# A decoder layer's attention sums as 64x64 tiles, two jobs moved from VectorE to ScalarE, and the order of all steps written out

## The chip, the cores and the metric

The kernel runs on one core of a Trainium2 chip. The metric is the device time in microseconds (us) of the whole launch. TensorE (PE in the profile) multiplies, VectorE (DVE) and ScalarE (ACT) work elementwise, GpSimd (POOL) does four small operations per norm, and SyncE (SP) issues the transfers.

## The reference, cut to what matters

A post-norm decoder layer on x of (16, 256, 256): three blocks, each `x = layernorm(x + block(x))`.

- **A, attention by moments.** `z = conv(x @ in_proj)`, a causal convolution of 4 taps. The value channels (256 = 32 heads of 8) are multiplied by 4 angles each; cosine and sine of that, times `poly(x) * p * time_weight`, are summed over the sequence (`cumsum`), divided by the summed weight, normalised by their mean square, multiplied by `W_re` and `W_im` (from 8x4 moments back to 8 channels within a head), gated with `silu`, and multiplied by `out_proj`.
- **B, cross attention by autocorrelation.** Fourier transforms of query and context, products, an inverse transform, the top 5 lags of each head and their softmax, applied to the values in the frequency domain.
- **C, feed-forward with 16 small experts.** `xV * cumsum(yW)`, weighted by a softmax over routed experts, times U, divided by the position.

## The kernel before, in words

The batch of 16 is worked off in 8 chunks of 2 sequences: 512 tokens, in tiles of 128 channels by 512 tokens. All of TensorE's large products are in float32; the compiler makes two passes of each (so one product of 512 columns is two MATMUL records).

Every step is a small function (`a_sums`, `b_spectrum`, `c_own`, ...) that exists on each engine that takes part. It waits on semaphores for what it needs and ticks its own; `Steps` counts these. On each engine all steps stand in one order, and an engine works strictly in that order. The order is given by one function `turn` for each engine, which is called NCHUNK + 3 or + 4 times with the chunks a, b, c, d (and e) shifted by one: in turn t it starts block A of chunk t, finishes A of chunk t-1, does B of t-1 and t-2 and C of t-2 and t-3. Below, "turn t" is the stretch from the first transpose of chunk t (`a_transpose(t, 0)`, L540) to that of chunk t+1; the last stretch runs from the transpose of chunk 7 to the end.

Block A has 8 units a chunk (UNITS = 2 halves of 128 channels x M = 4 angles), half by half: unit u is half u // 4, angle u % 4. For each:

- VectorE `a_fraction`: the angle in turns, rounded to an integer by writing it as int32 (`kturn`, L1431), then the fraction left (L1434);
- ScalarE `a_angles`: absolute value, sine, cosine into `sc` (4 slots, cosine and sine of 128x512 each);
- VectorE `a_moments` (times the weight `g`, L1454) and `a_scan` (running sum, L1462);
- TensorE `a_sums` (L585): two products of 128x128 weights `wy` by 128x512 of `sc`, added up in the PSUM bank Y of the half. `wy` is block diagonal, 8x8 for each head;
- ScalarE `a_squares` (L1049), VectorE `a_accumulate` (L1472); then once a chunk TensorE `a_squares` (L597, weights of 128x32), VectorE `a_weight` (L1482), ScalarE `a_norm` (logarithm, exponential, copy), VectorE `a_factor` (L1489), TensorE `a_factor` (L556), VectorE `a_heads`, TensorE `a_out` (L615).

At the end of each block VectorE adds the residual and takes mean and variance, GpSimd makes the reciprocal root (`rstd`, L1259 and L1262), and VectorE subtracts and multiplies in four instructions (`ln_apply`, L1518). TensorE's other large steps: `a_project` (L573), `b_transform` (L631), `b_spectrum` (L647), `b_corr` (L659), `b_back` (L691), `b_out` (L701 and L703), `c_transpose` (L714), `c_hidden` (L724), `c_logits` (L733, weights of 128x32 into two column groups in turn), `c_running` (L758), `c_own` (L767), `c_spread` (L775), `c_out` (L786 and L788). In the first turn TensorE and ScalarE also do 34 `fold` steps (L441, L952), which multiply weight matrices together once; 21 of them stand in one block between `a_project(0, 3)` and `a_sums(0, 0)`.

Of the kernel before, what the change touches and what calls it, by code (L numbers as in the profile page):

```python
# [25 lines left out]
ALU = mybir.AluOpType  # L26
# [25 lines left out]
C_ID, C_HS, C_HM, C_POS, C_RN, C_M0, C_E8, C_SG, C_LO, C_END = 0, 128, 192, 208, 464, 466, 468, 596, 598, 600  # L52
# [29 lines left out]
def each(kinds, over):  # L82
# [3 lines left out]
LAYER_NORM = each("res", range(2)) + each("stats aggr norm", range(NQ))  # L86
# [4 lines left out]
             + each("y", range(UNITS)) + ["S"] + each("fe out", range(2)))  # L91
VEC_A = Steps("vec_a", [("tap", j, t) for j in Z_ORDER for t in (2, 1, 0)] + [("stap", t) for t in (2, 1, 0)]
              + ["clip", "expo", "plow", "den", "guard", "w", "flow"]
              + each("p2 g both gf y", range(2)) + each("turns frac mom scan", range(UNITS))
              + [("acc", u) for u in range(UNITS) if u % M] + LAYER_NORM)
ACT_A = Steps("act_a", each("xT silu p1", range(2)) + ["zs", "exp", "phigh", "e", "ln", "f", "fhigh"]
              + each("z", Z_ORDER) + each("abs cos sin sq", range(UNITS)))
POOL_A = Steps("pool_a", ["var", "rstd"])
# [4 lines left out]
ACT_B = Steps("act_b", each("xf cf ot", range(2)) + SPEC + ["exp", "wt"])  # L103
POOL_B = Steps("pool_b", ["var", "rstd"])
# [6 lines left out]
ACT_C = Steps("act_c", each("xT", range(2)) + each("h", range(4)) + ["logit", "exp", "wT"] + each("c", range(NJ)))  # L111
POOL_C = Steps("pool_c", ["var", "rstd"])
# [5 lines left out]
BANK_A = {("xT", 0): 2, ("xT", 1): 1, ("zs",): 2, ("z", 0): 1, ("out", 0): 0, ("out", 1): 0, ("pe", 0): 2, ("z", 1): 1, ("pe", 1): 2, ("z", 2): 0,  # L118
          ("z", 3): 1, ("Y", 0): 2, ("Y", 1): 0, ("S",): 1, ("fe", 0): 1, ("fe", 1): 1}
# [28 lines left out]
def chunks(t, stages):  # L148

    return [t - n if 0 <= t - n < NCHUNK else None for n in range(stages)]  # L150


# [5 lines left out]
def decoder_kernel(nc, x, ctx_in, in_proj, conv_w, conv_b, theta, decay, anchor, score, deriv, norm_sc,  # L158
# [4 lines left out]
    with ctx:  # L163
# [11 lines left out]
        headm = cst[:, C_HM:C_HM + 16]  # L175
# [5 lines left out]
        psel = sb("psel", [P, 4, P], F32R)  # L181
# [12 lines left out]
        wy = sb("wy", [P, 2, M, P])  # L194
# [62 lines left out]
        rs = [sb(f"rs{n}", [P, 2, NQ]) for n in "abc"]  # L257
# [17 lines left out]
        pselraw = acc[:, 0, 0, :].rearrange("p (k n) -> p k n", n=P)  # L275
# [39 lines left out]
        LOADS_A += [(win[:, :, 0:2 * D], in_proj[:, 0:2 * D].rearrange("(t p) n -> p t n", p=P)),  # L315
                    (wsr[:, :, :], in_proj[:, 2 * D:2 * D + HEADS].rearrange("(t p) n -> p t n", p=P))]
        for j in range(4):
            LOADS_A += [(cw[:, j, :], conv_w[:, 0, j * P:(j + 1) * P].rearrange("a p -> p a"))]
        LOADS_A += [(cb[:, 0:4], conv_b[0:2 * D].rearrange("(t p) -> p t", p=P)),
                    (thn[:, :, :], theta[0, 0].rearrange("(t k) h m -> (k h) t m", t=2)),  # L320
                    ]
# [32 lines left out]
        def _(sp):  # L354
            for dst, src in LOADS_S:
                sp.dma_start(dst, src).then_inc(w_small, 16)
            for dst, src in LOADS_A[:2]:
                sp.dma_start(dst, src).then_inc(w_attn, 16)
            sp.dma_start(xa[:, :, :], rows(x, 0)).then_inc(xa_in, 16)
            for dst, src in LOADS_A[2:]:  # L360
                sp.dma_start(dst, src).then_inc(w_attn, 16)
# [6 lines left out]
            def load_residual(i):  # L368
                if not is_first(i):
                    sp.wait_ge(*VEC_A.at(i - 1, "norm", NQ - 1))  # L370
                sp.dma_start(xs_a[:, :, :], rows(x, i)).then_inc(xr_in, 16)
# [6 lines left out]
            def store(i):  # L378
                sp.wait_ge(*VEC_C.at(i, "norm", NQ - 1))
                sp.dma_start(rows(out, i), xs_c[:, :, :]).then_inc(stored, 16)  # L380
# [15 lines left out]
            for i in range(3, NCHUNK - 1):  # L396
                load_x(i + 1)
                load_residual(i)
                store(i - 3)
                load_ctx(i)  # L400
            load_residual(NCHUNK - 1)
            store(NCHUNK - 4)
            load_ctx(NCHUNK - 1)
            store(NCHUNK - 3)
            store(NCHUNK - 2)
            store(NCHUNK - 1)
# [20 lines left out]
        def _(pe):  # L427
# [126 lines left out]
            def spread_heads(o, h):  # L554
                for b in range(SEQ):
                    last = mm(o[:, b * L:(b + 1) * L], psel[:, 2 * h + b, :], pair[:, :], start=True, stop=True)  # L556
                return last

            @staged
            def a_spread(i, h):  # L560
# [4 lines left out]
                spread_heads(o, h).then_inc(*PE_A.tick("pe", h))  # L565
# [36 lines left out]
            def a_factor(i, h):  # L602
# [4 lines left out]
                spread_heads(o, h).then_inc(*PE_A.tick("fe", h))  # L607
# [13 lines left out]
            def b_transform(i, name, t):  # L621
# [4 lines left out]
                else:  # L626
                    pe.wait_ge(*VEC_A.at(i, "norm", NQ - 1))
# [81 lines left out]
            def c_transpose(i, t):  # L709

                pe.wait_ge(*VEC_B.at(i, "norm", NQ - 1))
# [79 lines left out]
            def turn(a, b, c, d):  # L791
                c_spread(d, 3)
                c_own(d, 3)
                c_running(d, 4)
                b_corr(c)
                a_sums(b, 6)
                if is_first(b):
                    for k in fold_part(6):
                        fold(k)
                c_spread(d, 4)  # L800
                a_sums(b, 7)
                if is_first(b):
                    for k in fold_part(7):
                        fold(k)
                c_own(d, 4)
                c_running(d, 5)
                c_spread(d, 5)
                c_own(d, 5)
                a_squares(b)
                c_running(d, 6)  # L810
                b_wt(c)
                c_spread(d, 6)
                a_factor(b, 0)
                c_own(d, 6)
                b_wf(c)
                a_factor(b, 1)
                a_transpose(a, 0)
                c_running(d, 7)
                c_spread(d, 7)
                a_transpose(a, 1)  # L820
                a_out(b, 0)
                a_scores(a)
                c_own(d, 7)
                a_project(a, 0)
                b_back(c, 0)
                b_back(c, 1)
                a_out(b, 1)
                b_out(c, 0)
                a_spread(a, 0)
                a_project(a, 1)  # L830
                b_out(c, 1)
                c_out(d, 0)
                c_out(d, 1)
                if is_first(b):
                    pe.wait_ge(folded, len(FOLD))
                    pe.wait_ge(ready, 2)
                b_transform(b, "cf", 0)
                a_spread(a, 1)
                a_project(a, 2)
                b_transform(b, "cf", 1)  # L840
                a_project(a, 3)
                if is_first(a):
                    for k in fold_part(None):
                        fold(k)
                c_transpose(c, 0)
                c_transpose(c, 1)
                b_transform(b, "xf", 0)
                b_transform(b, "xf", 1)
# [1029 lines left out]
```

## Time and profile before

| | us |
|---|---|
| three runs | 1075.76, 1076.63, 1078.91 (median 1076.63) |
| the profiled execution | 1077.53 |
| its span, first to last instruction | 1075.7 |
| PE busy (matmuls) | 960.7 (89% of the span) |
| DVE busy | 852.4 (79%) |
| ACT busy | 471.9 (44%) |
| POOL busy | 45.9 (4%) |
| mean granted TensorE clock | 0.963 of full speed |

The span leaves out 1.8 us of the profiled execution's own time; the median of the runs is 0.9 us above the span. Busy times are those of the profile: overlapping instructions of one engine are counted once. The ends of matmuls are modelled, so that a busy PE holds small gaps.

### The profile page before, as it was taken

How to read it: one execution, taken by the hardware profiler on the slowest of the kernel's cores; microseconds unless marked ns; L12 is line 12 of the kernel's file. 1: busy time of each engine (PE TensorE's matmuls, PEld its weight loads, DVE VectorE, ACT ScalarE, POOL GpSimd, SP SyncE). 2: the span in 40 equal slices, each digit the busy share in tenths (PEclk: the TensorE clock that was granted, in tenths of full speed). 3: DMA queues.
4: the chain of work that ended last, by engine and by line, in shares of the span. 5: the costliest groups of instructions: out<-in, count | busy, mean ns of one | idle time of the engine just before them, and what ended most of it. 6: DMA issues, size and time to landing. Idle time of an engine off the chain costs nothing. (4 is left out here: it accounts for less than half of the span.)

```text
span 1075.7 us, 10422 instructions
## 1 busy us (share of the span) xinstructions
PE 960.7 (89%) x3460; PEld 587.8 (55%) x3482; DVE 852.4 (79%) x1459; ACT 471.9 (44%) x736; POOL 45.9 (4%) x64
## 2 busy tenths in 40 slices
PE   2596685889999999999999999999999998998696
PEld 1253352655467545855485547754675467547245
DVE  3769699999997999799989999799979984173232
ACT  1465364268333943285328633583339411410310
POOL 0001000020001000100000000000010001000000
PEclk9799897899999999999999999999999999999789
DMA  7700010010001000010001000100010000000000
GB/s 211 164 1 0 20 39 1 20 39 1 0 21 41 19 1 21 1 59 0 20 1 59 1 0 21 59 1 1 1 52 8 1 1 20 1 0 1 19 1 20
DMA packets 38167, 25.45 MB, mean 24 GB/s; under 512 B 17991, under 2 KB 37474, under 8 KB 38114
## 3 DMA queue, kind: packets, MB, share of 16 engines
q1 hardware_dynamic: 38114, 24.78, 8.0%
q8 instruction: 29, 0.48, 0.2%
q14 instruction: 24, 0.20, 0.1%
HBM read 20.58 MB, written 4.19 MB: 23 GB/s over the span
## 5 line engine op out<-in xcount | busy, mean ns | idle before, releaser
L1462 DVE TENSOR_TENSOR_SCAN sc<-mask,sc 128x1024 f32<-128x1024 bf16 x64 | 146.2, 2284 | 0.1
L585 PE MATMUL ps<-sc,wy 128*128 128x512 f32 x256 | 126.2, 621 | 13.5 <-DVE sc L1462 10.8
L767 PE MATMUL ps<-x2t,mv 128*128 128x512 f32 x256 | 122.5, 601 | 3.2 <-DVE prod L1707 3.1
L758 PE MATMUL ps<-cum,mw 128*128 128x512 f32 x256 | 123.6, 606 | 1.2 <-ACT wparts L1136 1.2
L786 PE MATMUL ps<-up,prod 128*128 128x256 f32 x512 | 115.9, 379 | 0.9 <-DVE prod L1707 0.9
L786 PEld LDWEIGHTS ps<-up,prod 128*128 128x128 f32 x512 | 94.8, 190 | 13.8 <-issue 1.7
L1145 ACT ACTIVATE cs<-ps 128x512 f32<-128x512 f32 x64 | 37.7, 589 | 113.3 <-PE ps L758 112.5
L1454 DVE TENSOR_TENSOR sc<-sc,g 128x1024 f32<-128x1024 f32 x64 | 77.6, 1212 | 9.7 <-ACT sc L1030 9.5
L585 PEld LDWEIGHTS ps<-sc,wy 128*128 128x128 f32 x256 | 48.0, 195 | 66.0 <-issue 50.2
L758 PEld LDWEIGHTS ps<-cum,mw 128*128 128x128 f32 x256 | 47.5, 192 | 60.1 <-issue 59.7
L1375 DVE SCALAR_TENSOR_TENSOR zc<-ps,cw,zc 128x510 f32<-128x510 f32 (+2 forms) x96 | 71.0, 745 | 11.2 <-ACT zc L971 8.9
L767 PEld LDWEIGHTS ps<-x2t,mv 128*128 128x128 f32 x256 | 47.4, 191 | 57.6 <-issue 47.3
L573 PE MATMUL ps<-xt,win 128*128 128x512 f32 x128 | 67.3, 654 | 0.0
L1072 ACT ACTIVATE spec<-ps 128x512 f32<-128x512 f32 x32 | 18.8, 595 | 109.5 <-PE ps L631 109.2
L1699 DVE TENSOR_TENSOR cs<-cs,ps 128x512 f32<-128x512 f32 x64 | 43.6, 681 | 24.3 <-ACT cs L1145 14.6
L724 PE MATMUL ps<-x2t,mr 128*128 128x512 f32 x128 | 60.0, 614 | 0.8 <-ACT x2t L1105 0.8
L1049 ACT ACTIVATE sq<-sc 128x1024 f32<-128x1024 f32 x48 | 50.5, 1051 | 21.2 <-DVE sc L1462 21.2
L1472 DVE TENSOR_TENSOR acc<-acc,sq 128x1024 f32<-128x1024 f32 x48 | 58.6, 1220 | 0.6 <-ACT sq L1049 0.3
L1716 DVE SCALAR_TENSOR_TENSOR x<-ps,cst,x 128x256 f32<-128x256 f32 x32 | 14.0, 480 | 55.5 <-PE ps L788 55.5
L971 ACT ACTIVATE zc<-ps,cb,cw 128x512 f32<-128x512 f32 x32 | 24.8, 775 | 64.2 <-PE ps L573 64.1
L1707 DVE TENSOR_TENSOR prod<-cs,ps 128x512 f32<-128x512 f32 x64 | 43.7, 683 | 10.3 <-PE ps L767 9.9
L1019 ACT ACTIVATE hq<-frac 128x512 f32<-128x512 f32 x64 | 40.1, 627 | 23.6 <-DVE frac L1434 23.4
(253 smaller groups left out, 1628.3 us busy)
## 6 DMA issues: line engine op xcount, KB each, us to landing
xa<-in_x_dram SPq DMA_DIRECT2D x8, 512.0 KB, 3.9
xs_a<-in_x_dram SPq DMA_DIRECT2D x8, 512.0 KB, 3.8
cin<-in_ctx_dram SPq DMA_DIRECT2D x8, 512.0 KB, 5.6
out_dram<-prod SPq DMA_DIRECT2D x8, 512.0 KB, 4.8
win<-in_L_attn_in_proj_w_dram SPq DMA_DIRECT2D x1, 512.0 KB, 4.1
prod<-in_L_ffn_V_fwd_dram SPq DMA_DIRECT2D x2, 256.0 KB
prod<-in_L_ffn_W_fwd_dram SPq DMA_DIRECT2D x2, 256.0 KB
prod<-in_L_ffn_W_inv_exp_dram SPq DMA_DIRECT2D x2, 256.0 KB
```

Source lines behind the costliest of these rows:

```text
L573: last = mm(o, win[:, t, j * P:(j + 1) * P], xt[:, t, :], start=(t == 0), stop=(t == DT - 1))
L585: last = mm(y, wy[:, 1 - c, m, :], sc[:, u % 4, c, :], start=(m == 0 and c == 0), stop=(m == M - 1 and c == 1))
L724: last = mm(o, mr[:, t, br, r * P:(r + 1) * P], x2t[:, t, :], start=(t == 0), stop=(t == 1))
L758: last = mm(o, mw[:, t, br, c:c + P], cum[:, t, :], start=(t == 0), stop=(t == 1))
L767: last = mm(o, mv[:, t, br, c:c + P], x2t[:, t, :], start=(t == 0), stop=(t == 1))
L786: mm(d, prod[:, j, q * P:(q + 1) * P], up[:, j, :], start=(j == 0), stop=False)
L1049: A(dst, sc[:, u % 4, :, :], ACT.Square, scale=1.0 / math.sqrt(2.0 * HD * M))\
L1375: STT(o[:, :, s:L], z[:, :, 0:L - s], cw[:, j, tap:tap + 1], o[:, :, s:L], ALU.mult, ALU.add)\
L1454: TT(sc[:, s, :, :], sc[:, s, :, :], g[:, h, :].unsqueeze(1).broadcast_to([P, 2, T]), ALU.mult)\
L1462: V.tensor_tensor_scan(flat, mask[:, 0:2 * T], flat, 0.0, ALU.mult, ALU.add)\
L1472: TT(acc[:, h, :, :], acc[:, h, :, :], sq[:, u % 2, :, :], ALU.add).then_inc(*VEC_A.tick("acc", u))
L1707: TT(prod[:, j, :], cs[:, j % 2, :], ps[:, BANK_C[("x", j)], :], ALU.mult)\
```

## The change

1. **Sums as tiles.** `a_sums` takes an angle m of both halves at once: 8 products of 64x64 weights by 64x512, in the four quadrants of TensorE's array, instead of 4 products of 128x128. It runs 4 times a chunk instead of 8. The channel quarters are placed so that the lower 64 rows always write the bank of Y 0 and the upper 64 rows that of Y 1. Units are counted angle by angle (u = 2m + h), and the first half holds channel quarters 0 and 3, the second 1 and 2. The loads of `win`, `cw`, `cb` and `thn` are cut into pieces for that, and a second selection matrix `pouter` is made.
2. **Integer turns on ScalarE.** `kturn` is written by an ACTIVATE (Identity with a scale column) in the new `a_turns`; VectorE keeps the second half of `a_fraction`.
3. **The norms' last step on ScalarE.** `ln_apply` becomes four ACTIVATE (Identity, bias and scale columns) in `a_layer`, `b_layer`, `c_layer`; GpSimd makes the bias as well, four operations in place of two. Waits on "norm" go to ScalarE's semaphores.
4. **One order for all chunks.** `turn` is gone on each engine. All steps of all eight chunks are written out, in an order that differs from chunk to chunk; the folds are spread among them. SP's order of transfers stays nearly the same.

```diff
             @staged
-            def a_sums(i, u):
-                h, m = divmod(u, M)
-                if m == 0:
-                    free_a(i, "Y", h)
-                y = ps[:, BANK_A[("Y", h)], :]
-                pe.wait_ge(*VEC_A.at(i, "scan", u))
-                for c in range(2):
-                    last = mm(y, wy[:, 1 - c, m, :], sc[:, u % 4, c, :], start=(m == 0 and c == 0),
-                              stop=(m == M - 1 and c == 1))
-                last.then_inc(*PE_A.tick("y", u))
+            def a_sums(i, m):
+                if m == 0:
+                    free_a(i, "Y", 0)
+                    free_a(i, "Y", 1)
+                pe.wait_ge(*VEC_A.at(i, "scan", 2 * m))
+                pe.wait_ge(*VEC_A.at(i, "scan", 2 * m + 1))
+                for c in range(2):
+                    for h in range(2):
+                        for r in range(2):
+                            src, dst = slice(r * H, (r + 1) * H), slice((r ^ h) * H, ((r ^ h) + 1) * H)
+                            last = mm(ps[dst, BANK_A[("Y", r)], :], wy[src, 1 - c, m, :], sc[src, (2 * m + h) % 4, c, :],
+                                      start=(m == 0 and c == 0), stop=(m == M - 1 and c == 1))
+                last.then_inc(*PE_A.tick("y", m))
...
+            @staged
+            def a_turns(i, u):
+                m, h = divmod(u, 2)
...
+                if u >= 2:
+                    act.wait_ge(*ACT_A.at(i, "cos", u - 2))
...
+                A(kturn[:, u % 2, :], zc[:, h, :], ACT.Identity, scale=thn[:, h, m:m + 1]).then_inc(*ACT_A.tick("turns", u))
...
+            def ln_apply(i, k, xs, dst, OWN, POOL):
+                act.wait_ge(*POOL.at(i, "rstd", 3))
+                for q in range(NQ):
+                    A(dst[:, q, :], xs[:, q, :], ACT.Identity, bias=rs[k][:, 2, q:q + 1], scale=rs[k][:, 1, q:q + 1])\
+                        .then_inc(*OWN.tick("norm", q))
...
             def a_fraction(i, u):
-                TS(kturn[:, u % 2, :], zc[:, h, :], thn[:, h, m:m + 1], None, ALU.mult)\
-                    .then_inc(*VEC_A.tick("turns", u))
-                dve.wait_ge(*VEC_A.at(i, "turns", u))
+                dve.wait_ge(*ACT_A.at(i, "turns", u))
                 STT(frac[:, u % 2, :], zc[:, h, :], thn[:, h, m:m + 1], kturn[:, u % 2, :], ALU.mult, ALU.subtract)\
                     .then_inc(*VEC_A.tick("frac", u))
...
-            def ln_apply(i, k, xs, dst, VEC, POOL):
-                dve.wait_ge(*POOL.at(i, "rstd"))
-                for q in range(NQ):
-                    TS(dst[:, q, :], xs[:, q, :], mvr[k][:, q, 0:1], rs[k][:, 1, q:q + 1], ALU.subtract, ALU.mult)\
-                        .then_inc(*VEC.tick("norm", q))
```

On TensorE the new order around the end of chunk 6's block A is this (the same sort of place in each of chunks 3 to 6):

```
... c_running(4, 7) c_spread(4, 7) c_own(4, 7) a_sums(6, 1) b_back(5, 0) b_back(5, 1) c_out(4, 0) c_out(4, 1)
a_sums(6, 2) a_sums(6, 3) a_squares(6) b_out(5, 0) a_factor(6, 0) b_out(5, 1) a_factor(6, 1)
a_transpose(7, 0) a_transpose(7, 1) a_out(6, 0) a_scores(7) a_project(7, 0) b_transform(6, "cf", 0) a_out(6, 1) ...
```

and at the end: `... c_out(6, 0) c_out(6, 1) b_out(7, 0) b_out(7, 1) c_transpose(7, 0) ...`. In the first turn 9 folds stand before `a_sums(0, 0)` on TensorE, and on ScalarE 7 stand before `a_angles(0, 2)`, where it was all of the first 21.

## Rows read from the trace of the kernel before

**Rows 1.** The page: busy time of each engine, and TensorE's in 40 slices

```profile
PE 960.7 (89%) x3460; PEld 587.8 (55%) x3482; DVE 852.4 (79%) x1459; ACT 471.9 (44%) x736; POOL 45.9 (4%) x64
PE   2596685889999999999999999999999998998696
```

**Rows 2.** Windows by turn: length, busy time (and instructions) of each engine, clock

```profile
20.20:112.70 92.50, 68.27 (x201) 36.32 (x201) 66.84 (x86) 46.90 (x85) 5.41 (x5) 0.89 0.31 73
112.70:198.50 85.80, 60.69 (x196) 37.03 (x197) 77.15 (x111) 40.70 (x63) 1.22 (x2) 0.84 0.06 19
198.50:301.50 103.00, 96.32 (x336) 56.47 (x337) 97.92 (x157) 57.03 (x87) 5.58 (x4) 0.97 0.05 16
529.70:643.80 114.10, 111.71 (x420) 68.98 (x422) 104.31 (x177) 57.69 (x88) 4.80 (x6) 1.00 0.06 19
757.90:1075.70 317.80, 287.97 (x1063) 181.56 (x1069) 185.02 (x368) 94.60 (x145) 12.23 (x18) 0.96 0.03 11
```

**Rows 3.** Timeline, TensorE: start, length, then line, operation, shape and count

```profile
512.27 1.05 PE L659 MATMUL ps<-fidft,cspec 128*32 128x256 f32 x4
...
520.65 1.88 PE L767 MATMUL ps<-x2t,mv 128*128 128x512 f32 x4
...
522.46 1.06 PE L597 MATMUL ps<-acc,cst 128*32 128x256 f32 x8
...
523.46 1.98 PE L758 MATMUL ps<-cum,mw 128*128 128x512 f32 x4
```

**Rows 4.** The chain that ended last: start, length, what

```profile
1012.55 1.91 PE ps L733 x8
...
1032.84 1.72 PE ps L758 x4
...
1052.03 3.69 PE ps L786 x16
...
1067.44 0.89 DVE x L1716 x2
```

**Rows 5.** Groups by line and form, VectorE: busy, mean ns, idle before

```profile
L1431 DVE TENSOR_SCALAR hq<-zc,thn 128x512 int32<-128x512 f32 x64 | 30.8, 481 | 0.3
...
L1518 DVE TENSOR_SCALAR prod<-x,mvrc,rsc 128x256 f32<-128x256 f32 x32 | 11.1, 410 | 11.2 <-POOL rsc L1262 11.2
```

**Rows 6.** Groups by line and form, ScalarE

```profile
L1000 ACT ACTIVATE g<-zc,dw 128x512 f32<-128x512 f32 x16 | 12.9, 805 | 3.0 <-DVE zc L1375 3.0
...
L948 ACT ACTIVATE up<-ps,acol 128x256 f32<-128x256 f32 x4 | 1.9, 474 | 5.0 <-PE ps L441 5.0
```

**Rows 7.** Groups by line and form, GpSimd

```profile
L1262 POOL TENSOR_TENSOR rsc<-rsc,half_ 128x4 f32<-128x4 f32 x8 | 8.1, 1008 | 0.6
```

**Rows 8.** Waits in the first turn (20 to 112.7 us): us in total, times, longest

```profile
DVE sc L1454 <- ACT sc L1030: 9.5, 1, 9.5
```

**Rows 9.** Timeline: from the squares to the next step, and one `b_out` pair

```profile
525.52 0.42 DVE L1489 TENSOR_TENSOR pair<-den,pair 64x256 fp32r<-64x256 f32 x1
...
526.04 0.51 PE L556 MATMUL ps<-pair,psel 128*128 128x256 f32 x2
...
544.01 1.03 PE L701 MATMUL ps<-wos,spec 128*128 128x256 f32 x4
...
545.97 0.39 PE L556 MATMUL ps<-pair,psel 128*128 128x256 f32 x2
```

**Rows 10.** Timeline, SyncE in the first microseconds, and what VectorE does then

```profile
7.35 0.43 SPq L358 DMA_DIRECT2D win<-in_L_attn_in_proj_w_dram  x1
...
8.85 3.09 SPq L361 DMA_DIRECT2D cw<-in_L_attn_conv_w_dram  x4
...
11.98 1.10 SPq L361 DMA_DIRECT2D cb<-in_L_attn_conv_b_dram  x1
...
13.12 0.51 SPq L361 DMA_DIRECT2D thn<-in_L_attn_theta_dram  x1
...
15.38 0.17 DVE L1323 TENSOR_SCALAR thn<-thn 128x8 f32<-128x8 f32 x1
```

**Rows 11.** Timeline, TensorE before the last chunk's block C

```profile
999.26 1.97 PE L714 MATMUL ps<-cst,x 128*128 128x128 f32 x8 [6.49 <-DVE x L1518]
```

More of the change, by code:

```diff
@@ new lines, in _ @@
+            b_wt(0)
+            b_wf(0)
+            a_sums(1, 1)
+            a_sums(1, 2)
+            b_back(0, 0)
+            b_back(0, 1)
+            b_out(0, 0)
+            a_sums(1, 3)
+            b_out(0, 1)
+            a_squares(1)
+            a_factor(1, 0)
+            a_factor(1, 1)
+            a_transpose(2, 0)
+            a_transpose(2, 1)
+            a_out(1, 0)
+            a_scores(2)
+            a_out(1, 1)
+            a_project(2, 0)
+            c_transpose(0, 0)
@@ new lines, in _ @@
+            c_spread(1, 4)
+            c_own(1, 4)
+            b_wt(2)
+            b_wf(2)
+            c_running(1, 5)
+            c_spread(1, 5)
+            c_own(1, 5)
+            c_running(1, 6)
+            b_back(2, 0)
+            b_back(2, 1)
+            c_spread(1, 6)
+            c_own(1, 6)
+            c_running(1, 7)
+            a_sums(3, 1)
+            c_spread(1, 7)
+            c_own(1, 7)
+            b_out(2, 0)
+            b_out(2, 1)
+            c_out(1, 0)
+            c_out(1, 1)
@@ new lines, in _ @@
+            b_wt(3)
+            c_own(2, 5)
+            c_running(2, 6)
+            c_spread(2, 6)
+            b_wf(3)
+            c_own(2, 6)
+            c_running(2, 7)
+            a_sums(4, 1)
+            c_spread(2, 7)
+            c_own(2, 7)
+            b_back(3, 0)
+            b_back(3, 1)
+            c_out(2, 0)
+            c_out(2, 1)
+            a_sums(4, 2)
+            a_sums(4, 3)
+            a_squares(4)
+            b_out(3, 0)
+            a_factor(4, 0)
+            b_out(3, 1)
@@ new lines, in _ @@
+            b_wf(4)
+            c_own(3, 6)
+            c_running(3, 7)
+            c_spread(3, 7)
+            c_own(3, 7)
+            a_sums(5, 1)
+            b_back(4, 0)
+            b_back(4, 1)
+            c_out(3, 0)
+            a_sums(5, 2)
+            c_out(3, 1)
+            b_out(4, 0)
+            b_out(4, 1)
+            a_sums(5, 3)
+            a_squares(5)
+            b_transform(5, "cf", 0)
+            b_transform(5, "cf", 1)
+            a_factor(5, 0)
+            a_factor(5, 1)
@@ new lines, in _ @@
+            c_spread(4, 7)
+            c_own(4, 7)
+            a_sums(6, 1)
+            b_back(5, 0)
+            b_back(5, 1)
+            c_out(4, 0)
+            c_out(4, 1)
+            a_sums(6, 2)
+            a_sums(6, 3)
+            a_squares(6)
+            b_out(5, 0)
+            a_factor(6, 0)
+            b_out(5, 1)
+            a_factor(6, 1)
+            a_transpose(7, 0)
+            a_transpose(7, 1)
+            a_out(6, 0)
+            a_scores(7)
+            a_project(7, 0)
@@ new lines, in _ @@
+            c_own(6, 6)
+            c_running(6, 7)
+            b_back(7, 0)
+            c_spread(6, 7)
+            c_own(6, 7)
+            b_back(7, 1)
+            c_out(6, 0)
+            c_out(6, 1)
+            b_out(7, 0)
+            b_out(7, 1)
+            c_transpose(7, 0)
+            c_transpose(7, 1)
+            c_hidden(7, 0)
+            c_hidden(7, 1)
+            c_hidden(7, 2)
+            c_hidden(7, 3)
+            c_logits(7)
+            c_running(7, 0)
+            c_turn(7)
@@ L1241, in _ @@
+            c_logits(7)
+            c_exp(7)
+            c_weights(7)
+            c_tile(7, 0)
+            c_tile(7, 1)
+            c_tile(7, 2)
+            c_tile(7, 3)
+            c_tile(7, 4)
+            c_tile(7, 5)
+            c_tile(7, 6)
+            c_tile(7, 7)
+            c_layer(7)
         @block.gpsimd
```

2200 lines of the change are left out of this document (1820 added, 380 removed).

## The prediction, made before the changed kernel ran

> **What bounds the kernel now.** I read the page first. TensorE is busy 960.7 of 1075.7 us, VectorE 852.4 [rows 1]. TensorE's slices show where that share is an average: below 9 in the first eight slices and in some of the last seven, full in between [rows 1]. So I cut the span by turns and asked for the windows [rows 2]. The reader is to see three kinds of stretch.
>
> - The first two turns (92.5 and 85.8 us): TensorE 68.3 and 60.7 us busy, and that at a granted clock of 0.89 and 0.84; VectorE 66.8 and 77.2. No C work exists yet. VectorE with its waits sets the length.
> - The steady turns, four of 114.1 us (the one from 529.7 stands for them): TensorE 111.7 busy, VectorE 104.3, ScalarE 57.7. TensorE is the bound, idle 2.4 us a turn; VectorE has only 9.8 us of slack.
> - The last stretch, 317.8 us: TensorE 288.0 busy, VectorE 185.0. TensorE is idle 29.8 us, all of it in pauses between dependent steps.
>
> A microsecond taken from TensorE therefore counts in the turns from 198.5 on, one taken from VectorE in the first two.
>
> **The sums, before.** Two products are four passes of 512 columns, and four such passes take 1.72 us (L758) [rows 4]. A chunk has 8 units: 13.7 us of its 111.7.
>
> **The sums, after.** No row shows four quadrants at work, nor two row halves. What rows show is two column groups. `c_logits` has 8 passes of 512 columns with 32-column weights, in two column groups in turn, and takes 1.91 us (L733) [rows 4]: the time of four passes, not eight. `a_squares` has 8 passes of 256 columns, first the four of one group, then the four of the other, and takes 1.06 us, where `b_corr`'s 4 passes in one group take 1.05 [rows 3]. So column groups run fully side by side, each with its own moving data, whatever their order in the program. The new group is 16 passes over four quadrants, four in each: at least 1.72 us if all four run together; 3.44 if only two do; 6.88 if none. The number of instructions is hardly a limit: in those 1.06 us TensorE takes 8 loads and 8 matmuls, and at that rate 16 and 16 need 2.1 us, no more than I come to below. I take 1.72, by the nearness of the column rows.
>
> Going in and out of a tiled group costs. Between the start of L767 at 520.65 and the first pass of L758 after the tiled L597 (523.46, and 0.10 more, since its four took 1.98 instead of 1.88) lie 2.91 us, for four passes of 512 (1.72) and the time of four of 256 (0.86): 0.33 us lost [rows 3]. A new group costs 1.72 + 0.33 = 2.05, four a chunk 8.2. Gain: 13.7 - 8.2 = 5.5 us; as `a_sums(2)` and `a_sums(3)` stand together in the new order and share one switch, I take 5.7.
>
> The Trainium skill ("TensorEngine Tiling (Array Packing)", Key Properties) agrees that a change of tiling mode drains the engine and that 64x64 gives four independent tiles; its Gotcha 1 says that two row tiles can't write one PSUM bank at a time. Here the lower rows write only bank Y 0 and the upper ones only Y 1, so by that page nothing is in the way. Against the change speaks "TensorE: Matmul & The Clock Gate" (Part 3): matmuls start and end in strict program order. What that would make of the time is a rival below; the `a_squares` row, where the second group does not wait for the first one's four passes, does not bear it out.
>
> **VectorE.** The integer turns are 64 instructions with 30.8 us, 3.85 a turn; the norms three groups of 32 with 11.1, 11.0 and 11.0, 4.1 a turn [rows 5]. VectorE has 104.3 - 8.0 = 96.3 us a turn left.
>
> **ScalarE.** The turns become ACTIVATEs of 128x512. The nearest row with columns for scale and bias takes 805 ns (L1000) [rows 6]; 8 a turn are 6.4 us, and at the lowest nothing more than VectorE's 481 ns each, 3.8. The norms are 12 ACTIVATEs of 128x256 at some 474 ns (L948) [rows 6], 5.7 us. From 57.7 to about 70 of a turn: it doesn't bound. This is costed at nothing because ScalarE idles 56 us a turn; without that cover it would be 12 us a turn. What can show is latency: the last fraction of each unit now needs one ScalarE step more, queued among copies out of PSUM. There are two slots, and fractions stand two units ahead of the moments in both orders, so in a turn I cost it at 0, at most 0.8 a unit, 6 a turn.
>
> **GpSimd** makes two operations more per norm. The power takes 1.0 us [rows 7]; the two new ones multiply only, between 0.2 and 1.0 each. Norms of A and of most of B are covered by other TensorE work; the last B and the last C are not.
>
> **The order, steady turns.** C of a chunk now ends before the next transpose of A; before, its last experts, `c_out`, and B's `b_back` and `b_out` lay in the next turn. Per turn the work is the same: 111.7 - 5.7 = 106.0 us. Does the new order starve TensorE at the end of A, where less C is left to fill? From the squares (522.46) to the factor product (526.04) the round trip through VectorE and ScalarE takes 3.6 us [rows 3, 9]. Behind the squares now stands only `b_out(5, 0)`, 1.96 us (544.01 to 545.97) [rows 9], and the squares themselves take 1.06: about 0.6 us is left open, before `a_squares` perhaps as much for the last three accumulates. I take the idle time of before, 2.4, and 0.6: a turn of 109.0. Bounds: 106.6 (the join hidden) and 114.
>
> **The start.** The first transpose waits for VectorE's setup, which has to wait for the small loads: it reads `thn` at 15.38, the queue having issued the last at 13.12 [rows 10]. SP now issues `win` in four pieces (+3 x 0.43), `cw` in five (+0.8), `cb` in four, `thn` in three (+2 x 0.51), nine issues more. For `cb` I take four small ones of about 0.45 for one of 1.10, +0.7. Together +3.8; the smaller `wy` gives 0.3 back. First transpose at 20.2 + 3.5 = 23.7 (bounds 20.2, if the loads weren't late, and 26).
>
> **First turn.** 3.85 us of integer turns leave VectorE. VectorE also stood 9.5 us before a moment [rows 8], while ScalarE copied the block of 21 folds. With 7 folds ahead of `a_angles(0, 2)` most of that goes; what is late next is ScalarE itself, which has 47 + 6 us to do. I take 5.4 of it: 92.5 - 3.8 - 5.4 = 83.3 (bounds 79 and 92).
>
> **Second turn.** VectorE loses 5.2 us (turns, one norm), and gains the end of B (0), which lay in the next turn (`b_apply`, `b_mix`, residual, about 7). 85.8 + 1.2 = 87 (83 to 92).
>
> **Third turn.** It now holds all of C (0), like a steady one: 109, where it was 103.
>
> **The last stretch.** It no longer holds what of C (4) and B (5) was left at the transpose of chunk 7: one expert step (1.72 x 2 + 0.2), `c_out` from 1052.0 to 1067.4 [rows 4], `b_back` (16 passes of 256 columns, 3.5 as such passes of L786 take), `b_out` 2 x 1.96: 26.4 us. The sums give 5.7. The norm before the last C has a pause of 6.5 us already [rows 11], in which VectorE waited for `c_out(6)`; now it follows `b_out(7)` and is residual, statistics, GpSimd and four ACTIVATEs, about the same. The end: two GpSimd operations and slower norms, +2 in all. 317.8 - 26.4 - 5.7 + 2.3 = 288.0.
>
> **Sum.** 23.7 + 83.3 + 87 + 5 x 109 + 288 = 1027.0 us of span, against 1075.7. The runs' median stands 0.9 above the span, the profiled time 1.8: **1028 us** for the median, -4.5%.
>
> **Rivals.**
>
> - **Coupling (0.12).** The chain of A's steps sets the turn, not TensorE's sum: fractions late by ScalarE, accumulates late before the squares. For: VectorE's 96.3 us leave 10 to 13 of slack, queues are strict. Against: before, with 9.8 of slack, TensorE idled 2.4. At turns of 114, 5 x 5: 1053.
> - **Two quadrants at a time (0.07).** Only column groups overlap, row halves don't. Group 3.44 + 0.33: 1.72 more, 24 groups in the TensorE-bound turns (chunks 2 to 7): +41, 1069.
> - **Strict order (0.04).** Each product is two passes in one quadrant; if passes start in program order, a product's second pass holds up the next quadrant. Nine steps of 0.43 = 3.9 us and 0.33, 2.2 more than forecast: +52, 1080, no change. That would be the page's rule quoted above.
> - **One at a time (0.07, the case of slower).** If 64-row weights stop the overlap altogether, a group takes 6.88 + 0.33, 5.2 more: 24 x 5.2 = +124, 1152 us. From a group of about 4.1 us on (49 us of gain over 24 groups are 2.0 each) the change no longer pays. No row excludes it; the column rows speak against.
>
> **Numbers.** The forecast has 0.70; its own range is 1010 to 1044, from turns at 106.6 (-12) and first turns at their low bounds (-6), to turns of 111 (+10) and the others high. The range of 8 in 10 goes to 1062: it takes in coupling, not the quadrant rivals. A change within 0.3% can't be told from none here. Faster 0.89 (forecast, coupling, two at a time), same 0.04, slower 0.07.
>
> **What would show it.** Sums: the group of 16 passes in 1.7 to 2.1 us on the timeline; 3.4 or 3.9 or 6.9 name the rivals. Steady windows of 107 to 111 us with TensorE near 106 and VectorE near 96; if TensorE's busy time falls but the turn stays, it is coupling, and the waits before L597's and the sums' successors name the place. The first transpose near 23.7. VectorE's wait of 9.5 us gone. The last stretch near 288. The prediction is wrong if the sums don't overlap, or if the written-out order makes pauses that the join's arithmetic above doesn't see.

## The result, and the profile after

The changed kernel takes 1031.15 us (four runs, 1029.45 to 1032.04) against 1077.2 for the kernel before beside it: a ratio of 0.957, 95% interval 0.9549 to 0.9591. The forecast was 1028. The profiled execution has a span of 1030.3 us.

The page of the changed kernel: busy times, TensorE's slices, and the groups that answer to the changed lines.

```profile
PE 911.1 (88%) x3719; PEld 553.9 (54%) x3738; DVE 792.5 (77%) x1301; ACT 565.7 (55%) x902; POOL 44.7 (4%) x112
PE   0489945889999999989998999989999999999795
L610 PE MATMUL ps<-sc,wy 64*64 64x512 f32 x512 | 62.7, 614 | 2.6 <-DVE sc L2539 2.6
L1537 ACT ACTIVATE hq<-zc,thn 128x512 int32<-128x512 f32 x64 | 46.0, 721 | 5.2 <-DVE zc L2460 4.1
```

Against [rows 1] TensorE has lost 49.6 us of busy time, VectorE 59.9, and ScalarE has gained 93.8. The sums are now 512 passes, twice as many as the 256 before, with a busy time of 62.7 us in all (a "pass" is one MATMUL record); the slices look as they did, low at the start, full in the middle.

The windows, in the order of [rows 2]: the first two turns, turns three to seven in one row, the last stretch. TensorE's new line for the transpose is L562.

```profile
24.00:103.50 79.50, 60.47 (x233) 31.39 (x233) 62.31 (x78) 49.27 (x89) 0.00 (x0) 0.89 0.37 86
103.50:192.60 89.10, 60.41 (x264) 39.24 (x265) 77.34 (x108) 52.21 (x83) 4.11 (x9) 0.83 0.06 18
192.60:752.70 560.10, 536.93 (x2248) 328.71 (x2262) 483.05 (x763) 346.17 (x540) 22.22 (x56) 0.99 0.06 19
752.70:1030.30 277.60, 252.58 (x976) 154.09 (x980) 161.84 (x310) 116.18 (x186) 16.09 (x36) 0.97 0.04 12
```

| stretch | predicted | measured |
|---|---|---|
| to the first transpose | 23.7 | 24.0 |
| first turn | 83.3 | 79.5 |
| second turn | 87 | 89.1 |
| five turns | 545 | 560.1 |
| last stretch | 288 | 277.6 |
| span | 1027.0 | 1030.3 |

The last two rows must be read together. The new order does not repeat from chunk to chunk, and the transpose that I cut at stands at a slightly different place in each; the single turns are 113.0, 112.2, 107.7, 119.2 and 108.0 us. Over both stretches TensorE is busy 789.5 us where I had 786, and idle 48.2 where I had 47. The five turns alone have 6.9 us of busy time more than 5 x 106.0, and most of that is the clock. In the kernel before the steady turns stand at a granted clock of 1.00; here it is at the lower of its two levels in three stretches of these turns (193.0 to 196.4, 223.8 to 227.3 and 558.3 to 565.2), in which TensorE is busy 12.8 us. The last of them, with what TensorE did ahead of it:

```profile
554.25 1.89 PE L672 MATMUL ps<-wqs,spec 128*128 128x256 f32 x8
559.30 2.07 PE L672 MATMUL ps<-wks,spec 128*128 128x256 f32 x4 [3.16 <-ACT qkv L1604]
...
558.30:565.20 6.90, 5.90 (x15) 4.82 (x16) 6.83 (x6) 3.19 (x6) 0.00 (x0) 0.51 0.00 0
```

TensorE stood idle for 3.2 us from 556.1 on, and at the lower level four passes then take 2.07 us where eight took 1.89. Half of the 12.8 us, 6.4, is my estimate of what the lower clock adds to the busy time of the five turns.

The timeline of TensorE at two groups of sums: one alone between full products, two together ahead of the squares.

```profile
490.97 1.88 PE L783 MATMUL ps<-cum,mw 128*128 128x512 f32 x4
492.78 1.95 PE L610 MATMUL ps<-sc,wy 64*64 64x512 f32 x16
494.88 1.88 PE L792 MATMUL ps<-x2t,mv 128*128 128x512 f32 x4 [0.16 <-issue]
...
515.31 3.66 PE L610 MATMUL ps<-sc,wy 64*64 64x512 f32 x32
519.06 1.06 PE L622 MATMUL ps<-acc,cst 128*32 128x256 f32 x8
```

Sixteen passes of 512 columns end after 1.95 us, where four of 128x128 take 1.88: all four quadrants run at once. From the start of the group to that of the next full product are 2.10 us; two groups in a row take 3.66. The forecast said 1.72 and 0.33, together 2.05.

### The profile page after: what moved, and what is told of

Its sections match the earlier page's. It is cut to its first block, busy times and chain, and to the rows that moved or that the text cites. A ratio compares the mean times of both kernels' runs of the same rounds, so it can differ in the third digit from the quotient of the medians.

```text
span 1030.3 us, 11040 instructions
## 1 busy us (share of the span) xinstructions
PE 911.1 (88%) x3719; PEld 553.9 (54%) x3738; DVE 792.5 (77%) x1301; ACT 565.7 (55%) x902; POOL 44.7 (4%) x112
## 4 chain that ended last, share of the span: by engine, by line
PE 64%; DVE 15%; ACT 13%; issue 5%; SPq 1%; POOL 1%; DMA 0%; ACTq 0%; DVEq 0%; POOLq 0%
PE ps L811 9%; PE ps L792 9%; PE ps L783 9%; PE ps L672 7%; PE ps L610 4%; PE ps L595 3%; PE ps L640 3%; PE ps L716 3%; PE ps L463 3%; PE ps L656 3%; DVE zc L2460 2%; PE ps L726 2%; DVE sc L2539 2%; ACT x L1674 2%; ACT L1422 1%
## 5 line engine op out<-in xcount | busy, mean ns | idle before, releaser
L2460 DVE SCALAR_TENSOR_TENSOR zc<-ps,cw,zc 128x510 f32<-128x510 f32 (+2 forms) x96 | 71.3, 743 | 22.7 <-ACT zc L1484 20.3
L610 PE MATMUL ps<-sc,wy 64*64 64x512 f32 x512 | 62.7, 614 | 2.6 <-DVE sc L2539 2.6
L2511 DVE SCALAR_TENSOR_TENSOR frac<-zc,thn,hq 128x512 f32<-128x512 f32 x64 | 47.7, 745 | 7.9 <-ACT hq L1537 7.5
L1537 ACT ACTIVATE hq<-zc,thn 128x512 int32<-128x512 f32 x64 | 46.0, 721 | 5.2 <-DVE zc L2460 4.1
L1555 ACT ACTIVATE sc<-hq,quarter 128x512 f32<-128x512 f32 x64 | 45.4, 710 | 0.0
L1604 ACT ACTIVATE qkv<-ps 128x512 f32<-128x512 f32 x48 | 28.2, 593 | 28.9 <-PE ps L672 19.0
```

Source lines behind the costliest of these rows:

```text
L610: last = mm(ps[dst, BANK_A[("Y", r)], :], wy[src, 1 - c, m, :], sc[src, (2 * m + h) % 4, c, :], start=(m == 0 and c == 0), stop=(m == M - ...
L2460: STT(o[:, :, s:L], z[:, :, 0:L - s], cw[:, j, tap:tap + 1], o[:, :, s:L], ALU.mult, ALU.add)\
```

## The experiments

All are compared with the kernel before on the same chip. Unless another number is given, "the changed kernel" is 1031.15 us. The kernel before has medians of 1076.3 to 1078.0 us beside them, so that a difference between two of the experiments can be off by 1 to 2 us for that alone.

**e1, e2, e3, e4: one part undone, then three.** e1 makes the sums 128x128 again:

```diff
-                        for r in range(2):
-                            src, dst = slice(r * H, (r + 1) * H), slice((r ^ h) * H, ((r ^ h) + 1) * H)
-                            last = mm(ps[dst, BANK_A[("Y", r)], :], wy[src, 1 - c, m, :], sc[src, (2 * m + h) % 4, c, :],
+                        last = mm(ps[:, BANK_A[("Y", h)], :], wy[:, 1 - c, m, :], sc[:, (2 * m + h) % 4, c, :],
```

> The changed kernel with the moment sums as 128x128 products again (four per angle, block-diagonal weights of 128 columns, channels in their natural order); order of steps, turns and norms stay as changed. Theory A (the gain is TensorE's time in the sums): each of the 24 groups in the TensorE-bound turns goes from about 2.0 to 3.4 us, 5.7 us a turn, so 1031 + 34 = 1065 us, within 6. Rival B (the new order is what saves): at most 1045 us.

Measured: 1070.74 us (1069.73 to 1071.2), ratio 0.9943 (0.9929 to 0.9956). The tiles are worth 39.6 us, most of the gain, as the first theory said; it is 5.6 us more than it said. The windows of the full turns and the first one, cut like those of the changed kernel:

```profile
24.50:109.60 85.10, 65.45 (x200) 35.34 (x200) 62.44 (x78) 49.28 (x89) 0.00 (x0) 0.90 0.32 77
...
197.40:786.70 589.30, 569.47 (x2101) 348.42 (x2102) 484.17 (x763) 346.41 (x540) 22.16 (x56) 0.99 0.06 18
```

The five turns are 29.2 us longer, 5.8 a turn, which is the forecast's 5.7 (TensorE's busy time in them is 32.5 more). What comes on top is the first turn: it is 5.6 us longer, where I had given the tiles nothing. VectorE is as busy in it as in the changed kernel (62.44 and 62.31 us), TensorE 5.0 us more.

e2 puts the integer turns back on VectorE:

```diff
-                dve.wait_ge(*ACT_A.at(i, "turns", u))
+                TS(kturn[:, u % 2, :], zc[:, h, :], thn[:, h, m:m + 1], None, ALU.mult)\
+                    .then_inc(*VEC_A.tick("turns", u))
+                dve.wait_ge(*VEC_A.at(i, "turns", u))
```

> The changed kernel with the integer turns on VectorE again, directly before the fraction. Theory A (VectorE has slack in the full turns, none in the first two): VectorE gains 3.85 us a turn, which shows in the first two turns alone: 1031 + 4 to 8, so 1037 us. Rival C (coupled queues: every microsecond on VectorE shows): 1031 + 8 x 3.85 = 1062 us. Rival D (ScalarE's turns are late): no slower, 1025 to 1031 us.

Measured: 1037.26 us (1033.49 to 1038.53), ratio 0.9627 (0.9611 to 0.9644), 6.1 more. The first turn is 83.7 us instead of 79.5; over the five full turns nothing is lost (557.2 against 560.1):

```profile
24.00:107.70 83.70, 61.46 (x233) 32.39 (x234) 65.99 (x86) 44.13 (x81) 0.00 (x0) 0.88 0.34 80
...
196.60:753.80 557.20, 536.36 (x2261) 325.76 (x2262) 501.06 (x803) 320.36 (x500) 22.16 (x56) 1.00 0.06 19
```

The first theory holds for the first turn and for the full ones. The second turn is 88.9 us against 89.1, so that there the 3.85 us don't show. The trace is of the fastest execution (1033.49), 1.4 us of span above the changed kernel's; it can't place the rest of the 6.1.

e3 puts the norms back on VectorE (the four TENSOR_SCALAR of the diff above, with the two GpSimd operations of before):

> The changed kernel with the norms' last step on VectorE again (four TENSOR_SCALAR, two GpSimd operations), each placed about two steps behind its residual. Theory A: VectorE gains 4.1 us a turn within its slack; 1031 to 1037 us. Rival C (coupled queues): 1031 + 33 = 1064 us. Rival D (ScalarE's four slow activations and two more GpSimd operations are on the path before the last B and C blocks): faster, 1026 to 1029 us.

Measured: 1043.62 us (1041.82 to 1044.0), ratio 0.9688 (0.9675 to 0.9701), 12.5 more. Neither number. The five full turns take 568.7 us, 8.6 more, and the trace shows two places for it, of which this is one (PE and DVE, end of chunk 3's block A):

```profile
192.20:760.90 568.70, 540.10 (x2261) 330.47 (x2262) 501.10 (x819) 319.23 (x484) 17.81 (x28) 0.98 0.06 18
...
413.71 0.48 PE L578 MATMUL ps<-pair,psel 128*128 128x256 f32 x2
414.79 1.38 DVE L2550 TENSOR_SCALAR prod<-x,mvrc,rsc 128x256 f32<-128x256 f32 x4 [1.18 <-POOL rsc L2280]
416.35 1.38 DVE L2550 TENSOR_SCALAR x<-x,mvrb,rsb 128x256 f32<-128x256 f32 x4 [0.18 <-POOL rsb L2280]
...
418.38 0.79 PE L578 MATMUL ps<-pair,psel 128*128 128x256 f32 x2 [4.19 <-DVE zc L2529]
```

In this kernel I had put two norms between VectorE's steps `a_factor` and `a_heads`, and TensorE's second factor product waits for `a_heads`: 4.2 us here, 8.2 in the two places, where the changed kernel waits 1.6 us for it in the same turns. Behind each of the two pauses stand 6.8 us at the lower clock. So the 8.6 us price the places that I gave the norms in VectorE's order; what they would cost at better ones was not run.

e4 undoes all three at once:

> All three undone: 128x128 sums, integer turns and norms on VectorE; what is left of the change is the written-out order (and the more finely cut loads at the start). Theory A, by the terms of the prediction: start +3.5, first turn -5.4, second +6.4, third +11.7, four turns +0.6 each, last stretch -24.1, together -5.5: 1072 us, within 8. Rival B (the order saves most of it): at most 1050 us. Rival C (the order only works with a relieved VectorE): over 1080 us.

Measured: 1088.21 us (1087.12 to 1089.31), ratio 1.0106 (1.0092 to 1.012). The written-out order without the rest is slower than the turns, by 11.8 us and not faster by 5.5. (The 5.5 holds 2.3 us that the prediction gave to the norms; by its terms the order alone was to save 7.8.) The number is that of rival C, over 1080. Its windows:

```profile
24.60:110.80 86.20, 65.57 (x200) 35.28 (x200) 66.01 (x86) 44.30 (x81) 0.00 (x0) 0.86 0.35 77
110.80:203.70 92.90, 65.88 (x233) 42.88 (x234) 82.17 (x120) 45.34 (x71) 3.75 (x7) 0.85 0.06 18
203.70:799.40 595.70, 569.54 (x2100) 349.39 (x2101) 520.06 (x859) 294.44 (x444) 17.82 (x28) 0.99 0.05 17
799.40:1085.90 286.50, 262.77 (x950) 160.26 (x949) 177.66 (x354) 93.29 (x142) 12.95 (x18) 0.97 0.04 12
```

The five full turns average 119.1 us where my terms gave 114.7, 22.2 us more in all. TensorE is idle 26.2 us in them, 5.2 a turn against 2.4 in [rows 2]; that is half of the surplus. The other half is busy time: 569.5 us for 2100 passes, where five of the steady turns before are 558.5. One of the pauses, and the clock behind it:

```profile
684.68 0.80 PE L578 MATMUL ps<-pair,psel 128*128 128x256 f32 x2 [3.85 <-DVE zc L2459]
...
683.60:690.40 6.80, 5.70 (x18) 4.54 (x18) 3.08 (x6) 1.19 (x2) 0.00 (x0) 0.50 0.25 76
```

The granted clock is at the lower level in 15.6 us of these turns, TensorE busy in 14.3 of them; some 7 of the 11 us are an estimate from that. The pause itself is that of e3: the second factor product waits for VectorE, which does two norms first, and two such waits are 7.7 us in the five turns. That fits rival C. Yet with turns and norms off VectorE (e1) the full turns take 589.3 us, only 6.4 less, so that a relieved VectorE is the smaller part of the loss. The three parts undone singly cost 39.6 + 6.1 + 12.5 = 58.2 us, together 57.1: within this order they add up.

**e5, e6, e9, e12: the parts in the old order.** `turn` is back on every engine. e5 has the tiles alone, with the sums at the places of every second old one. e6 has all parts but the order. e12 has the two moves alone: `a_turns` right behind the angles two units earlier, and the three norms together:

```diff
+                c_layer(d)
+                b_layer(c)
+                a_layer(b)
                 b_transform(b, "cf", 1)
```

> The kernel before with the tiled sums alone, in the order by turns: units angle by angle, the sums at the places of every second old one, the first half's second fraction behind the second convolution; integer turns and norms stay on VectorE, the start has the finely cut loads. Theory A (the parts add up): 1076.5 less the 39.6 us that undoing the tiles cost, 1037 us. Rival C (with TensorE at 106 us a turn VectorE's 104.3 becomes the bound, and its waits stand on top): turns of 109 to 111 us, 1050 to 1060 us.

> All parts of the change except the order: tiles, integer turns and norms on ScalarE, but the steps in turns as before (the turns two units ahead of the angles, the norms' steps before the second context transform). Theory A (parts add up, and the written-out order by itself cost 11.8 us): 1031 - 12 = 1019 us. Rival B (the written-out order is needed to use what the moves free): 1035 us or more.

> The kernel before with only the integer turns and the norms' last step moved to ScalarE: 128x128 sums half by half, order by turns. Theory A (VectorE's time counts in the first two turns alone): -3.8, -5.2, +2 at the end, 1069 us. Rival C (each microsecond off VectorE counts): 1076.3 - 64 = 1012 us; by what undoing both cost in the changed kernel (18.6 us): 1058 us. Rival D (ScalarE's queue makes the fractions and the block inputs late): 1078 us or more.

Measured: e5 1150.25 us (1149.21 to 1150.82), ratio 1.068 (1.0662 to 1.0697); e6 1200.9 us (1197.9 to 1202.93), ratio 1.1142 (1.1117 to 1.1167); e12 1128.37 us (1128.13 to 1129.05), ratio 1.0471 (1.0453 to 1.0488). e5 is far above both of its numbers. e6 and e12 fall to the rivals that were open upwards (1035 or more, 1078 or more), far above where these begin. Against the kernel before beside it, the tiles alone cost 73.9 us in the old order, the two moves alone 50.5 and all three 124.6, where undoing them in the new order costs 39.6, 18.6 (6.1 and 12.5) and 57.1. No line here bears on e6 alone: what makes it the slowest stays open.

For e5 the trace says where. Its busy times, a steady turn, and two of its waits (ScalarE's and VectorE's timeline). In the steady turn of the kernel before the first is 1.2 us long and the second no longer than that:

```profile
PE 952.2 (83%) x3738; PEld 569.0 (50%) x3738; DVE 854.6 (74%) x1461; ACT 471.7 (41%) x736; POOL 47.0 (4%) x64
...
446.30:571.20 124.90, 110.92 (x455) 66.54 (x454) 104.72 (x177) 57.75 (x88) 4.80 (x6) 0.96 0.06 18
...
519.05 0.63 ACT L1053 ACTIVATE sc<-frac 128x512 f32<-128x512 f32 x1 [5.58 <-PE ps L615]
...
521.76 1.23 DVE L1502 TENSOR_TENSOR acc<-acc,sq 128x1024 f32<-128x1024 f32 x1 [6.29 <-ACT sq L1074]
```

The sine of unit 4 needs the slot of unit 0, which the first group of sums frees; a group now needs two scans, and its place in my order was behind the logits. ScalarE stands 5.6 us, and VectorE waits behind it for a square. The waits are not all: TensorE has the products of the changed kernel, but is busy 952.2 us with them instead of 911.1, at a mean granted clock of 0.929 instead of 0.963. e9 tests the wait: one step is moved up on TensorE.

```diff
+                a_sums(a, 0)
                 b_spectrum(b, "qb")
...
                 b_spectrum(b, "ka")
-                a_sums(a, 0)
```

> The tiled sums alone in turns as in e5, with the first group of a chunk one block earlier on TensorE, ahead of b_spectrum(qb), so that the sine of unit 4 no longer waits 6 us for it. Theory (that one wait, and the accumulate that waits behind it, made e5 slow): 125 us a turn become 113 or less, 1070 us or less. Rival (pairs of units don't fit the old order: transposes of logits and weights, expert steps and sums wait for each other as well): 118 us a turn or more, 1100 us or more.

Measured: 1102.02 us (1100.4 to 1102.6), ratio 1.0223 (1.0207 to 1.0238). The place of one step out of some sixty is worth 48.2 us. The total is the rival's (1100 or more), the turn of 117.1 us lies between the two (113 and 118). Moving that step gave back 48.2 of the 73.9 us, so the theory had named a large cause and not the only one; the turn is still longer than 114.1. The mean granted clock is 0.946 here and TensorE's busy time 935.4 us, 16.8 less than in e5: part of what the step is worth is the clock.

```profile
545.30:662.40 117.10, 108.50 (x455) 65.72 (x454) 104.60 (x177) 57.67 (x88) 4.80 (x6) 0.99 0.06 19
```

TensorE now has 8.6 us of idle time a turn and VectorE 12.5, neither is full. e12's turn shows the same kind of thing on ScalarE. Its window, ScalarE's timeline, and the convolution on VectorE that waits for it:

```profile
548.10:671.10 123.00, 115.38 (x423) 70.20 (x422) 96.69 (x157) 69.16 (x108) 6.02 (x12) 0.97 0.06 18
...
590.00 2.06 ACT L1164 ACTIVATE prod<-x,rsc 128x256 f32<-128x256 f32 x4
592.10 2.07 ACT L1164 ACTIVATE x<-x,rsb 128x256 f32<-128x256 f32 x4
594.21 2.07 ACT L1164 ACTIVATE x<-xs_a,rsa 128x256 f32<-128x256 f32 x4
...
597.14 0.77 ACT L973 ACTIVATE zc<-ps,cb,cw 128x512 f32<-128x512 f32 x1
...
597.94 2.31 DVE L1424 SCALAR_TENSOR_TENSOR zc<-ps,cw,zc 128x510 f32<-128x510 f32 x3 [5.50 <-ACT zc L973]
```

Three norms in a row hold ScalarE for 6.3 us, and behind them waits the copy that starts a convolution, for which VectorE stands 5.5 us. VectorE has 96.7 us of work, 7.6 less than in [rows 2], and the turn is 8.9 us longer, 3.7 of them busy time of TensorE at a granted clock of 0.97. That the place of the norms is the cause is read from the timeline; no run moved them. These four kernels say what a place costs, not what the best old order could do: it was not searched for.

**e7 and e8: what lets the quadrants run together.** e7 sends each half's products to its own bank, so that lower and upper rows write one bank in the same stretch of time; e8 orders the products quadrant by quadrant.

```diff
-                            last = mm(ps[dst, BANK_A[("Y", r)], :], wy[src, 1 - c, m, :], ...
+                            last = mm(ps[dst, BANK_A[("Y", h)], :], wy[src, 1 - c, m, :], ...
```

> The changed kernel with each half's products going to its own bank, so that the lower and the upper 64 rows write one PSUM bank in the same microsecond; the channel quarters of the outputs are mixed up by it, all the work is the same. Theory (row halves can't write one bank at a time): only two quadrants run together, a group takes 3.4 instead of 1.8 us, 24 groups in full turns, 1031 + 41 = 1072 us. Rival (banks don't matter): 1031 us.

> The changed kernel with the eight products of a group ordered quadrant by quadrant, cosine and sine part of one quadrant behind each other (four passes in a row to one quadrant). Theory A (quadrants run by themselves whatever the order): group of 1.8 us, 1031 us. Rival (passes start in program order, so a quadrant's next pass holds up the others): a group of 13 steps of 0.43, 5.6 us, 24 x 3.7 = +89 us, 1120 us.

Measured: e7 1030.24 us (1026.07 to 1030.52), ratio 0.9557 (0.9534 to 0.9581); e8 1030.99 us (1027.36 to 1032.53), ratio 0.9569 (0.9544 to 0.9594). Neither matters. A group of e7, which shares banks:

```profile
491.08 1.95 PE L610 MATMUL ps<-sc,wy 64*64 64x512 f32 x16
492.96 0.39 PE L800 MATMUL ps<-wparts,sel 128*128 128x512 bf16 x1
```

1.95 us again: two row halves wrote different partitions of one bank with no loss. e8's products are written with four passes to one quadrant in a row, and its 512 passes are busy 64.1 us against 62.7:

```profile
L610 PE MATMUL ps<-sc,wy 64*64 64x512 f32 x512 | 64.1, 620 | 2.6 <-DVE sc L2539 2.6
```

The records don't name the quadrant of a pass, so that this rests on the order in the program and on the time.

The Trainium skill ("TensorEngine Tiling (Array Packing)", Gotcha 1) says that row tiles can't access one PSUM bank at the same time. For this case e7 decides against it. The Trainium skill ("TensorE: Matmul & The Clock Gate", Part 3) also says that matmuls start and end in strict program order. By the estimate in e8's expectation a group would then take 5.6 us, and e8's busy time decides against that.

**e10 and e13: two corrections.** e10 lets ScalarE issue the 17 loads of attention's weights.

```diff
+            for dst, src in LOADS_A:
+                act.dma_start(dst, src).then_inc(w_attn, 16)
```

> The changed kernel with attention's 17 small loads issued by ScalarE's queue beside SyncE's, instead of behind 18 others. Theory (the first transpose at 24.0 waits for the last of these loads): it starts at 20.3, 1031.15 - 3.7 = 1027.5 us. Rival (the setup is late anyway, or ScalarE's own setup is now late): 1031 us or more.

Measured: 1027.08 us (1025.28 to 1031.02), ratio 0.9535 (0.951 to 0.956). The number fits, but the reason only in part: the first transpose starts at 23.0, not 20.3. The last of these loads is now issued at 10.1 instead of 17.1, and VectorE still gets past its wait at 18.40 only:

```profile
10.13 0.91 ACTq L1422 DMA_DIRECT2D cb<-in_L_attn_conv_b_dram  x1
16.06 0.23 DVE L2401 TENSOR_SCALAR dw<-x 128x3 f32<-128x3 f32 x1
...
18.40 0.17 DVE L2404 TENSOR_SCALAR thn<-thn 128x8 f32<-128x8 f32 x1 [1.93 <-DMA cb<-in_L_attn_conv_b_dram]
```

The rest of the 4.1 us lies within the spread of the runs, and the two intervals overlap, so that only this 1.0 us is shown. The wait for the loads is still 1.9 us long, and VectorE's own chain ahead of it now ends at 16.5 instead of 15.1.

e13 adds to e10 that the last chunk's B and C norms are done by VectorE, which has nothing else to do there:

```diff
+            dve.wait_ge(*ACT_C.at(NCHUNK - 2, "norm", NQ - 1))
+            last_norm(1, x1, x2, ACT_B, POOL_B)
...
+            last_norm(2, x2, xs_c, ACT_C, POOL_C)
```

> e10 with the norms of the last chunk's B and C blocks alone on VectorE, where nothing else runs. Theory (these two stand on the path to the end): four activations take 2.07 us, four TENSOR_SCALAR 1.38, and one GpSimd step of 0.33 drops out, 1.0 us each, so 1027.1 - 2.0 = 1025 us and the last chunk's transposes wait 1 us less. Rival (the path is elsewhere): 1027 us, the same wait.

Measured: 1023.84 us (1022.86 to 1029.79), ratio 0.9523 (0.9501 to 0.9544), the lowest median here; its interval lies just below the changed kernel's and overlaps that of e10, so that of the step from e10 only what the trace shows is certain. TensorE's pause before the last block C, first in the changed kernel, then in e13:

```profile
956.85 1.97 PE L739 MATMUL ps<-cst,x 128*128 128x128 f32 x8 [6.00 <-ACT x L1674]
```

```profile
948.99 1.94 PE L735 MATMUL ps<-cst,x 128*128 128x128 f32 x8 [5.04 <-DVE x L2593]
```

1.0 us less, as expected. It was 6.5 in [rows 11], where `c_out` came last.

## Why the prediction was right, and where only its sum was

- **The sums.** Right in kind and nearly in size: the four quadrants run together, 1.72 and 0.33 us were taken and 2.10 in all (1.83 a group in a row) measured. I counted the six TensorE-bound stretches and got 34 us; e1 gives 39.6. A full turn gains 5.8 us of its length, as forecast, but the first turn 5.6 instead of nothing: TensorE loses 5.0 us of busy time in it and VectorE nothing, so that I was wrong to call it VectorE's alone.
- **The three rivals on the quadrants** (two at a time, strict order, one at a time) are refuted by the timeline: 1.95 us, where they had 3.4, 3.9 and 6.9. e7 and e8 show that this hangs neither on the bank nor on the order that the change has chosen.
- **The moves.** Mis-sized: I had -3.8 in the first turn, -5.2 in the second, +2.3 at the end, together 6.7 us of gain. Going from e4 to e1, they are worth 17.5 us, by the windows 1.1 in the first turn, 5.1 in the second, 6.4 in the five full ones and 4.3 in the last stretch, where I had a loss. The integer turns behave as forecast in the first turn and the full ones (e2). The norms do not: "costed at nothing" in the full turns was wrong by 8.6 us over five (e3), at the places that they have there. ScalarE's own prices were off in both directions, 721 ns for a turn (taken 805) and 590 for a norm's activation (taken 474).
- **The order.** Wrong in sign. Without moves and tiles my terms for start, stretches and turns add up to about -8 us; e4 measured +11.8. Start and first two turns went as I said (203.7 us against 203.0), the last stretch is 4.9 shorter (286.5 against 291.4), the five full turns are 22.2 longer. Two steps failed there. One is "the idle time of before and 0.6": a full turn of the new order without the other parts has 5.2 us of TensorE's idle time, and in the changed kernel 4.6, not 3.0. The other is "per turn the work is the same": the passes are, their time is not, since part of them runs at the lower clock; 11.0 us more over e4's five turns, and 6.9 more than forecast in the changed kernel's. The cut between the last two stretches falls at another point of the work, but their sum is 17.3 us too long as well, 12.2 busy and 5.1 idle.
- **The sum** is right because these cancel: -39.6 - 17.5 + 11.8 = -45.3 measured, -34.2 - 6.7 - 7.8 = -48.7 forecast. The tiles are understood. That the error of the order (19.6) and those of moves and tiles (10.8 and 5.4) leave 3.4 us is luck. By the prediction's own signs the steady windows were to be 107 to 111 us, and it was to be wrong if the written-out order made pauses that its arithmetic didn't see; the single turns go up to 119.2, and it did make them.
- **Coupling**, the rival with 0.12: the five turns average 112.0 us, between the 109 of the forecast and its 114. Of these 3.0 us, 1.4 are busy time and 1.6 idle time. e3 shows that a few microseconds of VectorE count where a product of TensorE stands behind them in the chain; e2 puts 18 us more work on VectorE in these turns and does not lengthen them, which speaks against a chain that sets the turn. How much of the 1.6 us is coupling stays open.
- **The first turn**: VectorE's wait of 9.5 us [rows 8] is gone; its longest is 5.4 now. I had left 4 of these 9.5 in.
- **Slips of the prediction that change little.** TensorE's third slice in [rows 1] is 9, so that not all of the first eight are below it. In the second turn -5.2 and "about 7" give +1.8, and I used +1.2; 89.1 was measured for 87.
- **What I did not ask**: what each part does without the order. There the answer changes sign. e5, e6, e9 and e12 show that parts and order can't be priced apart, since the queues are strict: the tiles need two scans before a slot is free, the norms need ScalarE when it is not about to feed a convolution (read from the timeline alone). That the order shown was laid out for these parts is an inference from e4 against the others; a turn order tuned as carefully for them was not tried, so how much of the gain needs a written-out order stays open.

## What to carry to other kernels

When weights are block diagonal, count the passes by quadrant: eight 64x64 products in four quadrants cost as much as two 128x128 products plus some 0.4 us of change-over (2.10 against 1.72 us), and did so in both orders and on both choices of banks tried; they did the work of four. Price work moved to an idle engine by what stands behind it in that engine's queue at that place: the same moves gained 17 us in one order and cost 51 in another, and the place of one step was worth 48 us. Count a pause of TensorE more than once: the passes behind it can run at the lower clock, as they did for 12.8 us here. A total that comes out right is no proof of its terms; undoing the parts is what showed three of them off.

## What the runs showed of the hardware that was not expected

- Two 64-row tiles wrote different partitions of one PSUM bank in the same stretch of time without loss (1.95 us for 16 passes, e7).
- Behind a pause of 3.2 us TensorE's granted clock was 0.51 for 6.9 us, and passes took about twice as long (changed kernel, from 558.3 on); for the same products e5 is busy some 40 us more than the changed kernel.
- Four ACTIVATEs of 128x256 with bias and scale columns from SBUF take 2.07 us (mean 590 ns), VectorE's four TENSOR_SCALAR 1.38; an Identity that writes int32 takes 721 ns for 512 columns, less than the 805 of L1000, which has a bias column as well.
- Small loads issued 7 us earlier from a second queue were waited for only 1 us less (18.40 instead of 19.36).
